# Gated mLSTM attention with a mixture of eight experts: the last two batches drained in their own order, choice counts that compare with stored steps, the first expert's down weights split in block 0

## The chip, the cores and the metric

One core of a Trainium2 chip. The metric is the device time of one execution in microseconds (us); the median of the runs is given. Engines: TensorE (PE in the rows; PEld is its weight load), VectorE (DVE), ScalarE (ACT), GpSimd (POOL), SyncE (SP). All numbers of time below are from one profiled execution, counted from the start of its span.

## The reference

The input x has 32 batches of 512 rows of 512 numbers; ctx has the same shape. Cut to what matters:

```python
x = x + tanh(g_xattn) * mlstm(layernorm(x), ctx, ctx, ...)       # 8 heads of 64
x = x + tanh(g_ffn) * ffn(layernorm(x), Wr, br, W_up, b_up, W_down, b_down)

def ffn(x, ...):                       # 16384 rows, 8 experts
    xf = x.reshape(16384, 512)
    Sm = softmax(xf @ Wr + br)         # probabilities, 16384 x 8
    G_t, idx_t = top_k(Sm.T, 2048)     # each expert chooses 2048 rows
    mid = silu(tokens @ W_up[expert // 2] + b_up)      # 512 -> 1365
    out = mid @ W_down[expert] + b_down                # 1365 -> 512
    y = zeros.at[idx].add(G * out)
```

So each expert takes the 2048 rows in which its probability is largest (on equal values the earlier row), and the output adds what the experts give for a row. The experts can't start before the probabilities of all batches are there.

## The kernel before, in words

**Two stages.** `attention` (L89) works through the batches, `experts` (L1288) through 32 blocks of 512 chosen rows, four blocks (BPE) for each expert. Each stage is one block of five instruction streams, one for each engine, ordered by hand; between streams there are only semaphores. At the end of a stage all engines meet.

**Attention** is a software pipeline: iteration i loads and norms batch i, turns q and k of batch i-1 and computes its gates, does the decays, scores and products of batch i-2, weighs the result of batch i-3 and adds it to x on GpSimd (`weigh_heads` L206: times one factor per head; `weigh_columns` L214: times the output weights Wo, then the add into xs), norms batch i-4 again (`second_norm`, ACT) into xfb, turns it on TensorE (`turn_rows`) and ACT copies it to xfT (`turned_rows`), and computes logits and probabilities of batch i-5 (`logits`, `turn_logits`, `shifted_logits`, `exponentials`, `probabilities`). The loops run NB + 5 = 37 iterations; in the last ones only the tail of this list is live. One batch of square roots a round: `row_variances` on VectorE, `rsqrt_guess` (a logarithm and an exponential) on ACT, `reciprocal_roots` (three Newton instructions and the means) on VectorE. It serves the heads of batch i-3, the first norm of batch i and the second norm of batch i-4 together.

Two banks, T[0] and T[1], carry every small product of TensorE that another engine takes. `iteration_fills` (L159) lists, for each iteration, the fills in their order, who takes each, and which bank (its last number) it uses; TensorE waits before a fill until the last one of the same bank is taken. All four xfT fills of a batch stand on bank 0, after lt.

For the last batch, 31, GpSimd weighs tile 0 only and VectorE tiles 1 to 3 (`last_rows`, L877), in the middle of iteration 34, ahead of `shifted_logits` of batch 29. SP stores in every iteration, in this order: rows of batch i-4, probabilities of batch i-5, x of batch i-3.

**The choice** (class `Select`, L1113). An expert's 16384 probabilities lie as 128x128. The 2048th largest is found two bits at a time: `steps` lists a turn, seven rounds on the upper 16 bits of the number, eight on the lower, then ties, base and four row steps that make the list of row numbers. A round is `product` (TensorE adds the counts over the partitions) and `decide` (VectorE finds the new known value and counts again in `reach`):

```python
self.step(dve.tensor_scalar(self.cand[:, :], self.threes[:, :], float(1 << bit), known[:, 0:1], ALU.mult, ALU.add))
for j in range(3):
    ins = dve.tensor_scalar(self.hit[:, j, :], values, self.cand[:, j:j + 1], self.less[:, :], ALU.is_ge, ALU.add,
                            accum_out=self.count[:, j + 1:j + 2])
```

cand holds the known value plus one, two and three steps. After the last upper round the key of the lower rounds is made (L1240 to L1244). For expert 0 the whole choice runs ahead of block 0 with nothing else on TensorE. For the others each step is put between the down matmuls of the expert before (`next_steps`, L1346).

**Weights** (`Weights`). A piece is loaded by SP into one of two raw buffers (piece m waits until piece m-2 is split), split by ACT into a high part (`hi`) and by another engine into the rest (`lo`). Expert 0 has four up and six down pieces (`first_down` = 10); all ten are split during its choice, with `lo` on GpSimd. Expert 1 and later have their down pieces split in their first block, one after each of the first steps of the up loop, with `lo` on VectorE (`down_pieces`, L1333); `lay` (L1100) then moves rows of the last chunk by three DMAs.

**A block**: 132 up matmuls in 11 groups over three banks UP, silu on ACT, the split of its result on VectorE, then four down groups of 32 matmuls over two banks DN; bias and gate on VectorE; a scatter with add by GpSimd (L1405). The rows of the next block are gathered meanwhile (L1385).

## Time and profile before

| | us |
|---|---|
| runs, median of 3 | 3284.83 (3283.53 to 3833.15) |
| the profiled execution | 3284.7 |
| its span in the profile | 3283.0 |
| mean granted clock of TensorE | 0.975 |
| last products of the attention's batch 31 begin | 1151.48 |
| attention ends, the choice's block begins | about 1195.8 |
| first list of rows ready for the gather | 1247.7 |
| first up matmul | 1258.66 |

The profiled execution's time is the same measure as the runs'; its span is 1.7 us shorter and is what all rows refer to. Mean times of a group are in ns, everything else in us.

### The profile page before, as it was taken

The page shows a single profiled execution, that of the slowest core. Times are in us where ns is not written, and L with a number is a line of the kernel's source. Part 1 is how long each engine was busy: PE and PEld are TensorE (multiplying, and loading weights), DVE is VectorE, ACT ScalarE, POOL GpSimd, SP SyncE. Part 2 cuts the span into 40 slices and gives each one's busy share as a digit, 9 for nine tenths or more (in the row PEclk, how much of TensorE's full clock was granted, in tenths as well). Part 3 has the DMA queues.
Part 4 walks back from the last instruction along what each step waited for, and adds up shares of the span by engine and source line. Part 5 has one row for each costly group of instructions (what it writes and reads, how often), then busy time and mean ns, then how long its engine had stood idle before and what let it go on. Part 6 is the DMA issues. An engine that isn't in the chain of part 4 may idle for free.

```text
span 3283.0 us, 60869 instructions
## 1 busy us (share of the span) xinstructions
PE 3054.0 (93%) x24708; PEld 2412.5 (73%) x24708; DVE 1918.8 (58%) x5481; ACT 1140.0 (35%) x1964; POOL 1079.0 (33%) x1020
## 2 busy tenths in 40 slices
PE   5899899998999927999999999999999999999998
PEld 4677777777777715777778778777778778777786
DVE  4778888888888765544545544554553554553332
ACT  3566767667676631112112112112112112211210
POOL 4465656656566541211111111121111112112111
PEclk8899999999999958999999999999999999999999
DMA  3133343433434142213223222223123223222211
GB/s 108 53 135 113 121 140 117 139 110 121 140 118 141 69 120 56 42 37 78 35 47 100 37 48 74 35 45 102 35 35 72 49 38 96 51 35 52 55 32 25
DMA packets 140064, 250.70 MB, mean 76 GB/s; under 512 B 31456, under 2 KB 31456, under 8 KB 139784
## 3 DMA queue, kind: packets, MB, share of 16 engines
q1 hardware_dynamic: 106104, 170.80, 15.4%
q0 software_dynamic: 28672, 67.65, 11.7%
q10 hardware_dynamic: 5008, 8.36, 0.8%
q8 instruction: 195, 3.19, 0.4%
q14 instruction: 85, 0.70, 0.1%
HBM read 137.23 MB, written 101.19 MB: 73 GB/s over the span
## 4 chain that ended last, share of the span: by engine, by line
PE 60%; DVE 2%; DMA 1%; issue 0%; POOL 0%; ACT 0%; POOLq 0%; ACTq 0%
PE DN L1515 29%; PE UP L1489 28%; PE TT L1459 2%; DMA w_raw<-in_L_ffn_W_down 1%; DVE c_hit L1203 0%; DVE c_cand L1201 0%; PE c_bank L1195 0%; DVE down_lo L1097 0%; PE c_bank L1187 0%; ACT z L1431 0%; DMA xg<-rows_scratch,slots 0%; POOL out_x L1405 0%; DVE c_gained L1235 0%; DVE c_key L1241 0%; POOL xg L1385 0%
## 5 line engine op out<-in xcount | busy, mean ns | idle before, releaser
L1405 POOL DMA_INDIRECT out_x<-y,slots x128 | 201.3, 1573 | 1639.2 <-DVE y L1569 1639.2
L1515 PE MATMUL DN<-down_hi,mid_hi 128*128 128x512 f32 x1408 | 578.8, 411 | 0.0
L1489 PE MATMUL UP<-xT_hi,up_hi 128*128 128x512 f32 (+1 forms) x1408 | 553.9, 393 | 2.0 <-DVE xT_lo L1526 0.9
L1489 PE MATMUL UP<-xT_hi,up_lo 128*128 128x512 f32 (+1 forms) x1408 | 555.4, 394 | 0.0
L1489 PE MATMUL UP<-xT_lo,up_hi 128*128 128x512 f32 (+1 forms) x1408 | 552.0, 392 | 0.0
L1431 ACT ACTIVATE z<-UP,bup 128x512 f32<-128x512 f32 (+1 forms) x352 | 240.9, 686 | 868.6 <-PE UP L1489 843.1
L1515 PE MATMUL DN<-down_hi,mid_lo 128*128 128x512 f32 x1280 | 505.0, 395 | 0.0
L1515 PE MATMUL DN<-down_lo,mid_hi 128*128 128x512 f32 x1280 | 504.9, 394 | 0.0
L1545 DVE CAST mid_hi<-z 128x512 fp32r<-128x512 f32 (+1 forms) x352 | 151.6, 431 | 492.3 <-ACT z L1431 489.1
L1414 ACT ACTIVATE xT_hi<-TT 128x512 fp32r<-128x512 f32 x126 | 74.9, 595 | 704.7 <-PE TT L1459 683.2
L1489 PEld LDWEIGHTS UP<-xT_hi,up_hi 128*128 128x128 f32 (+1 forms) x1408 | 260.2, 185 | 69.2 <-ACT z L1431 4.8
L1489 PEld LDWEIGHTS UP<-xT_lo,up_hi 128*128 128x128 f32 (+1 forms) x1408 | 259.7, 184 | 66.8 <-issue 0.3
L1489 PEld LDWEIGHTS UP<-xT_hi,up_lo 128*128 128x128 f32 (+1 forms) x1408 | 259.9, 185 | 65.6 <-issue 0.5
L1515 PEld LDWEIGHTS DN<-down_hi,mid_hi 128*128 128x128 f32 x1408 | 265.6, 189 | 52.2
L1515 PEld LDWEIGHTS DN<-down_hi,mid_lo 128*128 128x128 f32 x1280 | 239.8, 187 | 58.4
L1515 PEld LDWEIGHTS DN<-down_lo,mid_hi 128*128 128x128 f32 x1280 | 241.0, 188 | 46.1
L1567 DVE TENSOR_TENSOR y<-DN,bdn 128x512 f32<-128x512 f32 x128 | 88.5, 691 | 308.3 <-PE DN L1515 307.5
L1547 DVE TENSOR_TENSOR mid_lo<-z,mid_hi 128x512 fp32r<-128x512 f32 (+1 forms) x352 | 244.0, 693 | 12.1
L211 POOL TENSOR_TENSOR nsb<-nsb,rr 128x512 f32<-128x512 f32 x125 | 126.9, 1046 | 361.2 <-DVE nn L874 361.2
L900 DVE SCALAR_TENSOR_TENSOR C<-QK,C 128x512 f32<-128x512 f32 x256 | 164.3, 683 | 2.4 <-PE QK L653 1.0
L817 DVE BATCH_NORM_STATS2 st<-xs 128x6 f32<-128x512 f32 x256 | 158.2, 681 | 4.1 <-POOL xs L222 2.1
L1385 POOL DMA_INDIRECT xg<-rows_scratch,slots x128 | 140.8, 1100 | 59.1 <-issue 38.4
(246 smaller groups left out, 5133.7 us busy)
## 6 DMA issues: line engine op xcount, KB each, us to landing
xs<-in_x SPq DMA_DIRECT2D x32, 1024.0 KB, 7.7
kraw<-in_ctx SPq DMA_DIRECT2D x32, 1024.0 KB, 6.5
out_x<-xs SPq DMA_DIRECT2D x32, 1024.0 KB, 5.3
rows_scratch<-xfb SPq DMA_DIRECT2D x32, 1024.0 KB, 4.3
w_raw<-in_L_ffn_W_down SPq DMA_DIRECT2D x40, 512.0 KB, 4.4
w_raw<-in_L_ffn_W_up SPq DMA_DIRECT2D x16, 682.5 KB, 4.2
mid_hi<-mid_hi ACTq DMA_DIRECT2D x32, 86.0 KB
mid_lo<-mid_hi ACTq DMA_DIRECT2D x32, 84.0 KB
```

Of the source, the lines that this page charges most:

```text
L211: ins = eng.tensor_tensor(n, n, spread(scale[:, j, :], 2, DH), ALU.mult)
L817: dve.bn_stats(st[:, which, j, :], src[:, j, :]).then_inc(s["dchain"], 1)
L900: dve.scalar_tensor_tensor(out=c, in0=QK[:, par, :], scalar=DH ** -0.5, in1=c, op0=ALU.mult, op1=ALU.mult)\
L1385: pool.indirect_dma_start(xg[:, t, :], None, rows_v, bass.IndirectOffsetOnAxis(ap=slots[:, 4 * n + t:4 * n + t + 1], axis=0)).then_inc(s_r ...
L1405: pool.indirect_dma_start(out_rows, bass.IndirectOffsetOnAxis(ap=slots[:, m:m + 1], axis=0), y[:, t, :], None, compute_op=ALU.add).then_in ...
L1414: act.activation(xT[0][:, c, :], turned(n, c)[:, :], ACT.Copy).then_inc(s["thi"], 1)
L1431: act.activation(z[0:r, k % 2, :], UP[k % 3][0:r, :], ACT.Silu, bias=bup[0:r, e // 2, f:f + 1]).then_inc(s["z"], 1)
L1489: mm = pe.matmul(UP[k % 3][0:r, :], weights.up[wa][:, c, f * P:f * P + r], xT[xa][:, c, :], start=first, stop=(c == CH - 1 and wa == 1))
L1515: mm = pe.matmul(DN[m % 2][:, :], lhs, rhs, start=first, stop=(f == FCH - 1 and lhs is parts[-1][0]))
L1545: dve.tensor_copy(mid[0][0:r, f, :], z[0:r, k % 2, :]).then_inc(s["hi"], 1)
L1547: dve.tensor_tensor(mid[1][0:r, f, :], z[0:r, k % 2, :], mid[0][0:r, f, :].bitcast(FP32), ALU.subtract)\
L1567: dve.tensor_tensor(y[:, t, :], DN[m % 2][:, :], bdn[:, e % 2, :], ALU.add).then_inc(s["yp"], 1)
```

## The change

It touches three places.

1. **The drain.** All loops of the attention run NB + 2 iterations; what came later is written out by hand for each engine, a being batch 30 and b batch 31. TensorE's fills of xfT alternate between the banks. VectorE multiplies batch 31 with Wo pair by pair before its square sums are complete (`weigh_early`), takes the statistics of batch 30 tile by tile as GpSimd adds them, and does the second norm of tiles 1 to 3 of batch 31 itself (`last_norm`); ACT does tile 0. SP's order is rows 30, x 31, probabilities 29, rows 31, probabilities 30 and 31.
2. **The choice.** A class `Steps` holds, for each round, its step and the three multiples of it (`gain`, `reach`); GpSimd fills it at the end of its attention stream. A compare becomes one instruction that subtracts the known value and compares with the stored multiple. `gained` compares the summed counts with K - 0.5 and adds the steps reached. The key is made in two instructions.
3. **The weights.** Only the four up pieces of expert 0 are split ahead; its six down pieces go through block 0 as those of the others through their first blocks, with `lay` there too.

```diff
+            if i == NB + 2:
+                plan = [("lg", b5, 0, "act", 1), ("lt", b5, 0, "dve", 0)] + [("xfT", b4, c, "act", c % 2) for c in range(CH)]
+            if i == NB + 3:
+                plan = [("lg", b5, 0, "act", 0), ("lt", b5, 0, "dve", 1)] + [("xfT", b4, c, "act", c % 2) for c in range(CH)]
...
             @block.sync
+                store_rows(NB - 2)
+                store_x2(NB - 1)
+                store_probabilities(NB - 3)
+                store_rows(NB - 1)
+                store_probabilities(NB - 2)
+                store_probabilities(NB - 1)
...
             @block.gpsimd
+                pool.wait_ge(s["rr"], NB + 3)
+                weigh_heads(step, pool, NB - 1, slice(0, 1))
+                add_rows(pool, NB - 1, 0).then_inc(s["x2"], 1)
+                pool.wait_ge(s["x2"], NB)
+                plan.fill(pool, low[:, :])
...
             @block.scalar
+                b, a = NB - 1, NB - 2
+                numerators(b, 3)
+                squares(b, 3)
+                logit_rows(a - 1)
+                rsqrt_guess(NB + 2)
+                exponentials(a - 1)
+                second_norm(a, (0, 1, 2, 3))
+                for c in range(CH):
+                    turned_rows(a, c)
+                rsqrt_guess(NB + 3)
+                second_norm(b, (0,))
+                logit_rows(a)
+                exponentials(a)
+                for c in range(CH):
+                    turned_rows(b, c)
+                logit_rows(b)
+                exponentials(b)
...
             @block.tensor
+                product(NB - 1, 3)
+                for b in (NB - 3, NB - 2, NB - 1):
+                    logits(b)
+                    turn_logits(b)
+                    if b < NB - 1:
+                        for c in range(CH):
+                            turn_rows(b + 1, c)
...
             @block.vector
+                def weigh_early(b, p):
+                    n = nsb[:, b % 2, :, 2 * p:2 * p + 2, 0:DH]
+                    w = Wo[:, 2 * p * DH:(2 * p + 2) * DH].rearrange("p (a d) -> p a d", d=DH)
+                    step(dve.tensor_tensor(n, n, spread(w, 1, TILES), ALU.mult))
...
+                def last_norm(b):
+                    dve.wait_ge(s["rr"], b + 5)
+                    wait_filled(dve, "xfT", b - 1, CH - 1)
+                    dve.wait_ge(s_rows, 16 * b)
+                    for j in range(1, TILES):
+                        ins = dve.tensor_scalar(xfb[:, j, :], xs[:, b % XBUF, j, :], rr[:, N2 + j:N2 + j + 1],
+                                                nn[:, TILES + j:TILES + j + 1], ALU.mult, ALU.add)
+                    ins.then_inc(s["xf2v"], 1)
...
+                b, a = NB - 1, NB - 2
+                weigh_early(b, 0)
+                weigh_early(b, 1)
+                square_sums(b, 2)
+                weigh_early(b, 2)
+                for j in range(TILES - 1):
+                    dve.wait_ge(s["x2t"], j + 1)
+                    row_stats(a, j)
+                dve.wait_ge(s["x2"], a + 1)
+                row_stats(a, TILES - 1)
+                square_sums(b, 3)
+                head_variances(b)
+                row_totals()
+                row_variances(NB + 2)
+                shifted_logits(a - 1)
+                weigh_early(b, 3)
+                reciprocal_roots(NB + 2)
+
+                last_rows(b)
+                for j in range(1, TILES):
+                    row_stats(b, j)
+                dve.wait_ge(s["x2"], b + 1)
+                row_stats(b, 0)
+                row_totals()
+                row_variances(NB + 3)
+                probabilities(a - 1)
+                reciprocal_roots(NB + 3)
+                last_norm(b)
+                shifted_logits(a)
+                probabilities(a)
+                shifted_logits(b)
+                probabilities(b)
...
 class Steps:
+    def fill(self, pool, draft):
+        step = Chain(pool, self.made)
+        step(pool.memset(self.gain[:, :, :], 0.0))
+        for r, (_, bit) in enumerate(self.rounds):
+            ins = pool.memset(self.gain[:, r, 1:4], float(1 << bit))
+        step(ins)
...
+        step(pool.tensor_tensor(self.reach[:, :, :], self.gain[:, :, 1:4], spread(self.threes[:, :], 1, len(self.rounds)), ALU.mult))
...
 class Select:
+    def count_reaching(self, dve, values, r):
+        for j in range(3):
+            ins = dve.scalar_tensor_tensor(out=self.hit[:, j, :], in0=values, scalar=self.plan.gain[:, r, 0:1],
+                                           in1=self.plan.reach[:, r, j:j + 1].to_broadcast([P, P]), op0=ALU.subtract, op1=ALU.is_ge,
+                                           accum_out=self.plan.count[:, j + 1:j + 2])
         ins.then_inc(self.asked, 1)
-        dve.memset(known[:, 1:4], float(1 << bit)).then_inc(self.own, 1)
...
+            known = plan.gain[:, r + 1, 0:1] if g else self.low[:, :] if kind == "upper" else self.tail[:, :]
+            step(dve.scalar_tensor_tensor(out=self.gained[:, :], in0=bank[:, 508:512], scalar=self.K - 0.5, in1=plan.gain[:, r, :],
+                                          op0=ALU.is_ge, op1=ALU.mult, accum_out=known))
...
+                step(dve.scalar_tensor_tensor(out=self.key[:, :], in0=upper, scalar=self.low[:, :], in1=self.wrap[:, :].to_broadcast([P, P]),
+                                              op0=ALU.subtract, op1=ALU.mult, accum_out=self.junk[:, 0:1]))
+                step(dve.scalar_tensor_tensor(out=self.key[:, :], in0=lower, scalar=1.0, in1=self.key[:, :],
+                                              op0=ALU.mult, op1=ALU.add, accum_out=self.junk[:, 1:2]))
...
-        first_down = weights.upto("down", 0)
+        first = weights.upto("up", 0)
...
-            return [] if n % BPE or e == 0 else list(range(weights.upto("down", e) - (FCH + 1) // 2, weights.upto("down", e)))
+            return [] if n % BPE else list(range(weights.upto("down", e) - (FCH + 1) // 2, weights.upto("down", e)))
...
-                weights.lay(act, 0)
...
-                        if at == FCH - 3 and n and n % BPE == 0:
+                        if at == FCH - 3 and n % BPE == 0:
                             weights.lay(act, e)
```

## Rows read from the trace of the kernel before

**Rows 1.** The page: TensorE's busy time, and its granted clock in 40 slices.

```profile
PE 3054.0 (93%) x24708; PEld 2412.5 (73%) x24708; DVE 1918.8 (58%) x5481; ACT 1140.0 (35%) x1964; POOL 1079.0 (33%) x1020
...
PEclk8899999999999958999999999999999999999999
```

**Rows 2.** Busy time by stage: drain, choice, experts (length, engines, clock, DMA, GB/s).

```profile
1151.48:1195.79 44.31, 16.93 (x176) 11.81 (x175) 20.68 (x57) 14.87 (x29) 7.17 (x6) 0.56 0.27 96
1195.79:1247.73 51.94, 4.43 (x26) 2.56 (x27) 44.98 (x187) 12.56 (x11) 27.08 (x22) 0.50 0.49 134
...
1258.66:3283.00 2024.34, 2013.17 (x9061) 1592.58 (x9061) 952.13 (x2692) 363.66 (x532) 338.03 (x252) 1.00 0.25 52
```

**Rows 3.** Timeline of PE in the drain: start, us, instruction [idle before <-releaser].

```profile
1169.42 1.09 PE L589 MATMUL T<-ident,xfb 128*128 128x128 f32 x4 [13.95 <-DVE lt L836]
...
1176.70 1.94 PE L598 MATMUL T<-xfT,Wr 128*32 128x128 f32 x32 [0.78 <-ACT xfT L409]
...
1183.37 1.12 PE L589 MATMUL T<-ident,xfb 128*128 128x128 f32 x4 [3.72 <-ACT xfb L457]
```

**Rows 4.** Timeline of DVE in the drain.

```profile
1154.19 2.48 DVE L817 BATCH_NORM_STATS2 st<-xs 128x6 f32<-128x512 f32 x4 [2.11 <-POOL xs L222]
...
1160.50 3.73 DVE L211 TENSOR_TENSOR nsb<-nsb,rr 128x512 f32<-128x512 f32 x3
1164.27 2.75 DVE L218 TENSOR_TENSOR nsb<-nsb,Wo 128x512 f32<-128x512 f32 x3
1167.05 1.90 DVE L222 TENSOR_TENSOR xs<-xs,nsb 128x512 f32<-128x512 f32 x3
...
1179.48 0.20 DVE L84 SCALAR_TENSOR_TENSOR tt<-vv,rr 128x40 f32<-128x40 f32 x1 [6.28 <-ACT rr L392]
...
1194.80 0.19 DVE L843 TENSOR_TENSOR sm_all<-ex,sx 128x32 f32<-128x32 f32 x1
```

**Rows 5.** Timeline of POOL in drain and choice.

```profile
1149.54 4.62 POOL L222 TENSOR_TENSOR xs<-xs,nsb 128x512 f32<-128x512 f32 x4
...
1198.15 1.84 POOL L1176 IOTA c_slot_row<- 128x2048 f16 x1
1201.55 6.08 POOL L1097 TENSOR_TENSOR up_lo<-w_raw,up_hi 128x1365 fp32r<-128x1365 f32 x2 [1.56 <-ACT up_hi L1091]
...
1217.57 2.34 POOL L1097 TENSOR_TENSOR down_lo<-w_raw,down_hi 128x1024 fp32r<-128x1024 f32 x1 [1.69 <-ACT down_hi L1091]
```

**Rows 6.** Chain of waits in the choice: start, us, what.

```profile
1217.65 2.42 DVE c_key L1241
...
1222.68 0.24 DVE c_cand L1201
...
1222.95 1.08 DVE c_hit L1203 x6
...
1224.50 0.24 DVE c_cand L1201
```

**Rows 7.** DVE groups by form in the choice: count, busy us, mean ns, idle before.

```profile
L1201 DVE TENSOR_SCALAR c_cand<-c_threes,c_gain 128x3 f32<-128x3 f32 x15 | 13.4, 893 | 0.5
```

**Rows 8.** DVE groups by form from 1262 us to the end.

```profile
L1203 DVE TENSOR_SCALAR_CACHE_REDUCE c_hit<-c_key,c_cand,c_less 128x128 f16<-128x128 f32 x168 | 59.4, 404 | 2.1
...
L1241 DVE SCALAR_TENSOR_TENSOR c_key<-c_V,c_gain 128x128 f32<-128x128 uint16 x7 | 2.4, 341 | 0.0
```

**Rows 9.** Timeline of ACT in block 4.

```profile
1525.16 1.06 ACT L1091 ACTIVATE down_hi<-w_raw 128x1024 fp32r<-128x1024 f32 x1 [3.70 <-DMA w_raw<-in_L_ffn_W_down]
```

**Rows 10.** Busy time in expert blocks 0, 1, 4 and 16, as rows 2.

```profile
1258.66:1323.73 65.07, 65.07 (x285) 50.82 (x286) 32.51 (x116) 10.44 (x17) 8.72 (x7) 0.97 0.19 37
1323.73:1386.83 63.10, 63.10 (x286) 49.43 (x284) 32.51 (x122) 9.85 (x15) 10.88 (x8) 1.00 0.20 37
1512.42:1575.90 63.48, 63.44 (x286) 49.45 (x284) 38.15 (x120) 14.88 (x21) 11.65 (x8) 1.00 0.39 96
2268.74:2332.34 63.60, 63.60 (x285) 49.47 (x284) 38.14 (x120) 14.88 (x21) 11.65 (x8) 1.00 0.37 90
```

More of the change, by code:

```diff
@@ L219, in weigh_columns, with add_rows @@
             step(ins)
-            for j in range(tiles.start, tiles.stop):
-                xb = xs[:, b % XBUF, j, :].rearrange("p (h d) -> p h d", d=DH)
-                ins = eng.tensor_tensor(xb, xb, nsb[:, b % 2, j, :, 0:DH], ALU.add)
-            return ins
+        def add_rows(eng, b, j):
+            xb = xs[:, b % XBUF, j, :].rearrange("p (h d) -> p h d", d=DH)
+            return eng.tensor_tensor(xb, xb, nsb[:, b % 2, j, :, 0:DH], ALU.add)
         with nc.Block() as block:
@@ L1132, in __init__ @@
         self.groups = [list(range(a, a + TILES)) for a in range(0, self.KC, TILES)]
-        self.steps = [("turn", 0)] + [("upper", k) for k in range(self.TOP_BIT - self.LOWER - 1, -1, -2)] \
-            + [("lower", k) for k in range(self.LOWER - 2, -1, -2)] + [("ties", 0), ("base", 0)] \
-            + [("rows", g) for g in range(len(self.groups))]
-        self.V = sb("V", [P, P]); self.key = sb("key", [P, P]); self.beyond = sb("beyond", [P, P])
+        self.rounds = [("upper", k) for k in range(self.TOP_BIT - self.LOWER - 1, -1, -2)] \
+            + [("lower", k) for k in range(self.LOWER - 2, -1, -2)]
@@ new lines, in __init__ @@
+        self.steps = [("turn", 0)] + self.rounds + [("ties", 0), ("base", 0)] + [("rows", g) for g in range(len(self.groups))]
+        R = len(self.rounds)
+        self.gain = sb("gain", [P, R, 4]); self.reach = sb("reach", [P, R, 3])
+        self.threes = sb("threes", [P, 3])
+        self.count = sb("count", [P, 4], BF16)
+        self.onesb = sb("onesb", [P, P], BF16)
+        self.made = ctx.enter_context(nc.semaphore("c_made"))
+    def fill(self, pool, draft):
[3 more added lines that the diff above has]
+            ins = pool.memset(self.gain[:, r, 1:4], float(1 << bit))
+        step(ins)
+        step(pool.iota(self.threes[:, :], pattern=[[1, 3]], base=1, channel_multiplier=0, allow_small_or_imprecise_dtypes=True))
+        step(pool.tensor_tensor(self.reach[:, :, :], self.gain[:, :, 1:4], spread(self.threes[:, :], 1, len(self.rounds)), ALU.mult))
+        pool.memset(self.count[:, 0:1], float(P)).then_inc(self.made, 1)
+        step.line.n += 1
+        step(pool.memset(draft, 1.0))
+        step(pool.tensor_copy(self.onesb[:, :], draft))
@@ L1226, in decide @@
         if kind == "turn":
-            step(dve.memset(self.gain[0][:, :], 0.0))
             step(dve.tensor_copy(self.V[:, :], bank[:, 0:P]))
             if e == 0:
-                dve.wait_ge(self.made, 5)
-            self.reach(dve, upper, self.gain[0], self.steps[i + 1][1])
+                dve.wait_ge(plan.made, plan.MADE)
+            self.count_reaching(dve, upper, 0)
         elif kind in ("upper", "lower"):
-            old, new = self.gain[(i - 1) % 2], self.gain[i % 2]
-            dve.wait_ge(self.own, step.line.n)
@@ L1243, in decide @@
[L1243 to L1248 removed]
+                if e == 0:
+                    dve.wait_ge(self.laid, self.LAID)
@@ L1388, in _ @@
                 select.constants(pool)
-                for m in range(first_down):
+                for m in range(first):
                     weights.lo(pool, m)
@@ L1414, in turn_hi @@
                     act.activation(xT[0][:, c, :], turned(n, c)[:, :], ACT.Copy).then_inc(s["thi"], 1)
[L1416 removed]
+                for m in range(first):
                     weights.hi(act, m)
```

174 lines of the change are left out of this document (87 added, 87 removed).

## The prediction, made before the result was known

> **What bounds the kernel now.** I read the page first, then busy time by stage, then the chain of waits, then the timelines of single engines between 1149 and 1262 us. The page shows TensorE at 93% and at full clock nearly everywhere, except for one slice of half clock between 1149 and 1231 us [rows 1]. The stages say where that lies [rows 2]. From 1258.66 us to the end TensorE is busy for 2013 of 2024 us: the expert stage is bound by its matmuls, and no edit changes their number. The 44.3 us before 1195.79, in which the last batches of the attention drain, hold 16.9 us of TensorE work, and the 51.9 us after it, in which the first expert's rows are chosen, hold 4.4. Those 96 us are latency: a gain or a loss there moves the end one for one. The change touches both, and the first expert block behind them.
>
> **Drain of the last two batches.** Behind the logits of batch 29 TensorE stands still for 13.95 us, until 1169.42, when VectorE has taken them (L836) [rows 3]. VectorE has them late in its order: it first weighs and adds three tiles of batch 31, from 1160.50 to 1168.9 [rows 4]. Then the four turns of batch 30 go one at a time, because all use one bank: 7.3 us from 1169.42 to the logits at 1176.70, 1.80 each where TensorE's share is 1.1 [rows 3]. ACT takes up the guess for batch 31's norm only after them, so VectorE waits 6.28 us for it [rows 4].
>
> The new order, worked forward:
> - The roots of round NB+2 are ready at 1160.5 now [rows 4]. Ahead of them VectorE gets three early products with Wo, and one behind the variances, and they alternate with GpSimd's four adds, which run from 1149.5 [rows 5]: a tensor_tensor of VectorE on two SBUF tiles takes 1.24 beside GpSimd (3.73 for 3) and 0.63 alone [rows 4, 5]. The row statistics now start tile by tile instead of after all four adds. Stepping through it, the roots come 1.1 us later: 1161.6.
> - Batch 31's three tiles: the products with Wo (2.75) are gone from there. Left are 3.73 for the head weights, 1.9 for the adds, and 0.6 for meeting GpSimd's add and its new fills: 1167.8.
> - Statistics 2.48, totals and variances 0.6: 1170.9. ACT's guess follows at once, since batch 30's copies are over by then (norm of 30 until 1164.6, with 3.0 for its four rows as from 1180.4 to the turn at 1183.37 now, four turns at about 1.1 each on two banks): 0.55, and the Newton steps 0.9: 1172.4. So the 6.28 us wait is gone.
> - Three rows of the last norm on VectorE, about 0.5 each (the 0.49 of L1569, same shape and operation), beside one on ACT: 1173.9. That batch 30's logits (about 1.9, from 1169.7) and their turn are done by then costs nothing; the store of batch 30, for which the last norm also waits, is issued at 1164.6.
> - From batch 31's first turn to its last probability it takes 11.6 now (1183.37 to 1194.99) [rows 3, 4]. Two banks save three times 0.7: 9.5. End 1183.5 instead of 1195.0.
>
> That is 11.5 us gained. If the alternation costs each DVE product one more GpSimd instruction, 8 are left; if turns pair up better and the early products cost nothing, 14.
>
> **The choice of the first expert.** A round is a count on VectorE, a 4-column matmul and a decision, with 15 rounds in it. An unhindered round takes 1.82 us, from one candidate instruction (1222.68) to the next (1224.50), and 1.08 of it are the three compares [rows 6]. The change:
> - takes the candidate instruction out of every round: 15 x 0.27 = 4.0 gained;
> - with it go its stalls. The 15 candidates took 13.4 us together [rows 7], 9.8 more than 15 x 0.24. They ended when a GpSimd instruction ended (the long iota, the splits up_lo and down_lo) [rows 5];
> - makes the key in two instructions instead of copy, three 128x128 passes and a memset. Now this is 5.2 us, from 1217.49 to 1222.66, 2.42 of them in one scalar_tensor_tensor that started with GpSimd's split at 1217.57 [rows 5, 6]; with nothing beside it the same instruction takes 0.34 [rows 8]. New: 2 x 0.45. 4.3 gained;
> - but makes each compare a scalar_tensor_tensor with two SBUF tiles. The old compare ran through splits untouched (0.40 with 0.33 between starts, in every case [rows 8]); the new one has the form of c_key, the one that was blocked. So GpSimd's splits now stop the compares, nearly from beginning to end: 6.08 for two up pieces, then 2.6 and 2.6, and perhaps the iota, 1.84 [rows 5]. The six down pieces are no longer there. Stepping the rounds through these windows (one compare gets in between two splits) I get 9.4 without the iota and 11.0 with it: given back.
>
> With the iota 4.0 + 9.8 + 4.3 - 11.0 = 7.1, and a little more for the memset ahead of the first count; without it 8.7. I take 8.0, between the two. Bounds: compares that are not blocked, 18; compares at half pace, 0.13 each more for their 128 elements, 45 x 0.13 = 6 less: 2.
>
> The Trainium skill bears on two of these steps. "SBUF — State Buffer" (section "SBUF: two separate sides") says that VectorE with two SBUF inputs and a GpSimd instruction that reads SBUF exclude each other for a whole instruction; c_key at 2.42 beside 0.34 agrees, and the iota, which reads nothing, would by this rule stop no compare: by it the choice gains 8.7 rather than 7.1. "Vector Engine (DVE) Microarchitecture Reference" (section "Points that are easy to get wrong") says that a scalar_tensor_tensor with two SBUF sources that aren't bf16 runs at half throughput, since no port is left for the accumulator. The trace has no such instruction with an accumulator; c_key without one, 0.34, isn't halved.
>
> GpSimd's constants for the counts move into the drain, where it idles from 1165 us on: nothing gained but 0.1, since the first product came right behind the first count anyway.
>
> **The first expert's down weights.** Their six pieces leave the choice and are split by ACT and VectorE in block 0, as in the first block of every other expert. There ACT waits on loads (3.70 us before the third piece, [rows 9]), yet the blocks take 63.48 and 63.60 us where one without pieces takes 63.10 [rows 10]; two others were at 63.1. TensorE has three output banks ahead of it, and that hides it. Block 0 begins at half clock and takes 65.07 now [rows 10], which slows its demand, not its loads. I take 0.3 lost, between 0 and 1.5. The seven later choices run beside the down matmuls, which wait for no count today; 0.27 off each decision changes nothing.
>
> **Sum.** 11.5 + 8.0 - 0.3 = 19.2. The profiled execution took 3284.7 (span 3283.0 and 1.7 around it), so it goes to 3265.5; the median of the three runs, 3284.83, lies 0.1 above it: 3265.6.
>
> **Rivals.**
> - Free compares (0.1): they pass the splits as the old ones did. For it speaks that both have an accumulator and that 45 old ones were never blocked; against it the 2.42 of c_key. Choice 18 instead of 8: 3255.6.
> - Half-pace compares (0.12): 6 more in the choice, 3271.6. This is the page's rule above.
> - The drain yields half (0.12): ACT or TensorE, in a strict order of their own, become late where I have them idle, or two SBUF products meet more of GpSimd: 5.7 instead of 11.5, 3271.4.
> - Slower than before (0.02): block 0 starves. Two raw buffers carry six pieces, so the last two pairs each pay a full load. It decides from the point where a load takes longer than the cover; beyond it each us of load costs about 2. For 19.2 lost a load must take some 10 us more than the 7 behind the 3.70 us wait, with block 0 at 85 us and the whole at 3286 or more. The other first blocks, with scatter and gather beside their loads, speak against it.
>
> **How the numbers follow.** The forecast has 0.64, the rivals 0.36 together. For the forecast alone the range is 3261 to 3270. Taking in the half-pace and the half-drain case with a little beyond, and the free compares, gives 3255 to 3274. A change of over 2% (about what a measurement of this kernel can tell from none) would need 66 us of the 96, or as much lost: 0.01 each, and 0.98 for within.
>
> **What would show it.** Right: in the drain the gap of TensorE after the logits of batch 29 ends with the norm of batch 30, near 1165, turns come 1.1 apart, and attention ends near 1183.5. In the choice, compares of 2.5 to 3 us stand exactly where GpSimd's four up_lo lie, and the others are 0.33 apart; the first gather is issued near 1228. Block 0 takes 65 to 66 us, and all later blocks are as they were. Wrong: compares 0.45 apart or more, roots of round NB+2 beyond 1163, block 0 over 67 us, or any later block longer.

## The result and the profile after

| | before | after |
|---|---|---|
| runs, median | 3283.53 (3279.67 to 3833.15, five) | 3258.58 (3256.45 to 3259.18, five) |
| ratio, with its 95% interval | | 0.9926 (0.991 to 0.9941) |
| the profiled execution, its span | 3284.7, 3283.0 | 3257.32, 3255.4 |
| mean granted clock of TensorE | 0.975 | 0.98 |

The change takes 24.95 us off the median, 0.74% by the ratio: within 2%, but well clear of no change by the interval. Of the five runs of before, 3833.15 was a slow one; without it their median is 3282.76 and the gain 24.2. The forecast was 3265.6; the result lies 7.0 below it, inside the wide range of 3255 to 3274 but below the 3261 to 3270 given for the forecast alone. It is nearer to the rival of free compares (3255.6), so the time alone would have pointed to the wrong mechanism; the profile decides. The spans of the two profiled executions differ by 27.6, and that is what the account below divides. The boundaries in the table are starts of instructions in the timelines, and for block 0 the end of its last matmul.

| stage | before | after | gained | forecast |
|---|---|---|---|---|
| start to the last products of batch 31 | 1151.48 | 1150.84 | 0.64 | 0 |
| drain, to the choice's first turn | 44.35 | 30.54 | 13.81 | 11.5 |
| choice, to its first list of rows | 51.65 | 40.71 | 10.94 | 8.0 |
| first list to first up matmul | 11.18 | 10.90 | 0.28 | 0 |
| block 0 | 65.07 | 63.33 | 1.74 | -0.3 |
| the rest | 1959.27 | 1959.08 | 0.19 | 0 |

The page of after, answering [rows 1]: TensorE's busy time and its granted clock in 40 slices.

```profile
PE 3048.6 (94%) x24708; PEld 2411.2 (74%) x24708; DVE 1870.8 (57%) x5235; ACT 1140.2 (35%) x1961; POOL 1064.8 (33%) x1029
...
PEclk8899999999999969999999999999999999999999
```

Busy time by stage in after, answering [rows 2] and [rows 10]: drain, choice, block 0, all experts (length, PE, PEld, DVE, ACT, POOL, clock, DMA share, GB/s).

```profile
1150.84:1181.38 30.54, 14.60 (x177) 11.46 (x176) 21.39 (x60) 12.79 (x26) 8.72 (x27) 0.64 0.39 139
1181.38:1222.09 40.71, 4.24 (x23) 2.29 (x23) 34.46 (x154) 6.65 (x5) 14.10 (x11) 0.50 0.39 103
1232.99:1296.32 63.33, 63.33 (x285) 49.80 (x286) 35.80 (x110) 15.63 (x23) 9.35 (x7) 1.00 0.34 82
1232.99:3255.40 2022.41, 2011.39 (x9061) 1592.46 (x9061) 912.03 (x2474) 369.88 (x538) 334.87 (x252) 1.00 0.25 53
```

TensorE's busy share hardly moves (93 to 94%), and its expert work is as long as it was (2013.17 and 2011.39). Where before has two slices at 5 and 8, one at 6 is left: the low stretch is shorter, not gone. Of the 27.6 us, 24.75 lie in the two stages in which TensorE mostly waits, and 1.7 where the first block starts; the 0.64 and 0.19 at both ends are no more than single executions differ by.

TensorE in the drain of after, from its timeline, answering [rows 3] (start, us, instruction, idle before it and what ended it).

```profile
1162.71 3.77 PE L638 MATMUL T<-ident,xfb 128*128 128x128 f32 x16 [7.88 <-ACT xfb L485]
...
1171.35 0.45 PE L655 MATMUL T<-ident,lg 128*128 128x128 f32 x1 [3.01 <-ACT lg L495]
1171.69 3.74 PE L638 MATMUL T<-ident,xfb 128*128 128x128 f32 x16
1176.21 1.94 PE L647 MATMUL T<-xfT,Wr 128*32 128x128 f32 x32 [0.78 <-ACT xfT L437]
```

The gap of 13.95 us before batch 30's turns is 7.88 and ends with ACT's norm of batch 30, as forecast. The four turns go as one group of 16 transposes in 3.77: 0.94 apart where they were 1.80.

VectorE in the drain of after, from its timeline, answering [rows 4].

```profile
1148.79 2.27 DVE L938 TENSOR_TENSOR nsb<-nsb,Wo 128x512 f32<-128x512 f32 x2
...
1151.69 0.96 DVE L938 TENSOR_TENSOR nsb<-nsb,Wo 128x512 f32<-128x512 f32 x1
...
1158.10 0.68 DVE L938 TENSOR_TENSOR nsb<-nsb,Wo 128x512 f32<-128x512 f32 x1
...
1159.72 3.73 DVE L223 TENSOR_TENSOR nsb<-nsb,rr 128x512 f32<-128x512 f32 x3
1163.48 2.05 DVE L236 TENSOR_TENSOR xs<-xs,nsb 128x512 f32<-128x512 f32 x3
...
1170.14 1.46 DVE L967 TENSOR_SCALAR xfb<-xs,rr,nn 128x512 f32<-128x512 f32 x3
...
1180.35 0.19 DVE L900 TENSOR_TENSOR sm_all<-ex,sx 128x32 f32<-128x32 f32 x1
```

The first two early products take 2.27 together (the second alone 1.55), the third 0.96, the fourth 0.68. The fourth is issued between variances and roots, and batch 31's tiles begin right behind it, at 1159.72. No wait of 6.28 us stands before the Newton steps any more: batch 31's norm starts at 1170.14, and its last probability ends at 1180.54.

GpSimd in drain and choice of after, from its timeline, answering [rows 5].

```profile
1148.89 5.94 POOL L236 TENSOR_TENSOR xs<-xs,nsb 128x512 f32<-128x512 f32 x4
...
1182.43 1.84 POOL L1313 IOTA c_slot_row<- 128x2048 f16 x1
1187.57 6.13 POOL L1215 TENSOR_TENSOR up_lo<-w_raw,up_hi 128x1365 fp32r<-128x1365 f32 x2 [3.29 <-ACT up_hi L1209]
1195.96 2.60 POOL L1215 TENSOR_TENSOR up_lo<-w_raw,up_hi 128x1365 fp32r<-128x1365 f32 x1 [2.26 <-ACT up_hi L1209]
1199.65 2.61 POOL L1215 TENSOR_TENSOR up_lo<-w_raw,up_hi 128x1365 fp32r<-128x1365 f32 x1 [1.09 <-ACT up_hi L1209]
```

VectorE in the choice of after, from its timeline: the compare beside the long iota, the three that met a split, and the first key instruction.

```profile
1182.47 0.35 DVE L1343 SCALAR_TENSOR_TENSOR c_hit<-c_V,c_gain,c_reach 128x128 f16<-128x128 uint16 x1
...
1187.77 3.01 DVE L1343 SCALAR_TENSOR_TENSOR c_hit<-c_V,c_gain,c_reach 128x128 f16<-128x128 uint16 x1
...
1190.71 3.13 DVE L1343 SCALAR_TENSOR_TENSOR c_hit<-c_V,c_gain,c_reach 128x128 f16<-128x128 uint16 x1
...
1196.01 2.69 DVE L1343 SCALAR_TENSOR_TENSOR c_hit<-c_V,c_gain,c_reach 128x128 f16<-128x128 uint16 x1
...
1199.75 2.66 DVE L1379 SCALAR_TENSOR_TENSOR c_key<-c_V,c_low,c_wrap 128x128 f32<-128x128 uint16 x1
```

This is the picture to learn. The compare at 1182.47 lies inside GpSimd's iota (1182.43 to 1184.27) and takes 0.35. The compares at 1187.77 and 1190.71 start in the pair of splits that begins at 1187.57 and ends at 1193.70, and take 3.01 and 3.13, to the end of the one split and to the end of the other; the compare at 1196.01 and the key at 1199.75 end with the next two splits.

VectorE's groups by form in the expert stage of after, answering [rows 8] (count, busy us, mean ns).

```profile
L1343 DVE SCALAR_TENSOR_TENSOR c_hit<-c_key,c_gain,c_reach 128x128 f16<-128x128 f32 x168 | 50.3, 350 | 2.0
...
L1379 DVE SCALAR_TENSOR_TENSOR c_key<-c_V,c_low,c_wrap 128x128 f32<-128x128 uint16 x7 | 2.5, 352 | 0.3
```

The new compare with nothing beside it takes 350 ns with its accumulator, the old one 404.

### The profile page after: what moved, and what is told of

Its sections match the earlier page's. It is cut to its first block, busy times and chain, and to the rows that moved or that the text cites. A ratio compares the mean times of both kernels' runs of the same rounds, so it can differ in the third digit from the quotient of the medians.

```text
span 3255.4 us, 60512 instructions
## 1 busy us (share of the span) xinstructions
PE 3048.6 (94%) x24708; PEld 2411.2 (74%) x24708; DVE 1870.8 (57%) x5235; ACT 1140.2 (35%) x1961; POOL 1064.8 (33%) x1029
## 4 chain that ended last, share of the span: by engine, by line
PE 60%; DVE 1%; DMA 1%; issue 0%; ACT 0%; POOL 0%; POOLq 0%; ACTq 0%
PE DN L1647 30%; PE UP L1621 28%; PE TT L1594 2%; DMA w_raw<-in_L_ffn_W_down 1%; DVE c_hit L1343 1%; PE c_bank L1336 0%; DVE down_lo L1215 0%; PE c_bank L1326 0%; ACT z L1566 0%; DMA xg<-rows_scratch,slots 0%; POOL out_x L1541 0%; DVE c_key L1379 0%; DVE c_gained L1372 0%; POOL xg L1521 0%; DVE mid_lo L1679 0%
## 5 line engine op out<-in xcount | busy, mean ns | idle before, releaser
L1647 PEld LDWEIGHTS DN<-down_lo,mid_hi 128*128 128x128 f32 x1280 | 241.2, 188 | 45.8
L702 PE MATMUL QK<-qT,kT 64*128 64x128 f32 x2048 | 153.2, 290 | 1.6 <-DVE C L988 1.6
```

Of the source, the lines that this page charges most:

```text
L702: mm = pe.matmul(QK[:, par, jj], kT[r, b % 2, p, jj], qT[r, b % 2, p, jj], start=True, stop=True)
L1647: mm = pe.matmul(DN[m % 2][:, :], lhs, rhs, start=first, stop=(f == FCH - 1 and lhs is parts[-1][0]))
```

## The experiments

Stage lengths of every run, read at the same instructions as above. The time is that of the profiled execution; single executions of the kernel before took 3278.5 and 3279.0 beside e1 to e7, and the median of 25 was 3283.65 beside e8 to e11.

| run | drain | choice | list to up | block 0 | span | time |
|---|---|---|---|---|---|---|
| before | 44.35 | 51.65 | 11.18 | 65.07 | 3283.0 | 3284.7 |
| after | 30.54 | 40.71 | 10.90 | 63.33 | 3255.4 | 3257.3 |
| e1_drain_alone | 29.36 | 48.12 | 11.04 | 65.22 | 3262.7 | 3264.6 |
| e2_ten_pieces | 30.53 | 49.01 | 11.10 | 64.91 | 3267.1 | 3269.0 |
| e3_old_choice | 30.36 | 45.81 | 10.93 | 64.88 | 3261.9 | 3263.9 |
| e4_one_bank | 34.34 | 40.14 | 10.95 | 63.42 | 3260.8 | 3262.7 |
| e5_wo_late | 30.58 | 40.16 | 11.01 | 63.32 | 3306.4 | 3308.4 |
| e6_psum_table | 30.52 | 30.46 | 10.88 | 63.40 | 3244.8 | 3246.8 |
| e7_before_warm | 44.31 | 51.90 | 10.92 | 64.87 | 3284.0 | 3286.1 |
| e8_before_warm2 | 44.30 | 49.17 | 11.57 | 63.28 | 3281.8 | 3283.5 |
| e9_psum_warm | 30.53 | 30.45 | 11.57 | 63.31 | 3247.1 | 3249.2 |
| e10_psum_table_timed | 30.53 | 30.46 | 10.84 | 63.38 | 3245.1 | 3247.1 |
| e11_psum_warm_all | 28.75 | 30.47 | 11.62 | 63.32 | 3241.9 | 3243.9 |

In e5 the attention ahead of the drain ran 47 us longer in this execution; its stage lengths are used, its time is not. The 3243.9 of e11 is the shortest of its 12 executions.

Each stage length is that of one execution, so its spread has to be known. The choice of after took 40.71, 40.16 and 40.14 in three runs that have the same choice (after, e5, e4), and that of e6 took 30.45 to 30.47 in four. The old choice with ten pieces took 48.12 to 51.90 in four; the reason is below.

**e1_drain_alone.** The attention of after without the constants of part 2 (`Steps.fill`), and everything behind the attention as in before.

```diff
-def attention(nc, io, NB, dram, sm_all, tg, consts, stored, plan):
+def attention(nc, io, NB, dram, sm_all, tg, consts, stored):
...
-                plan.fill(pool, low[:, :])
```

> The first part alone, the choice and the weights as before. If the three parts add up, the stage from the last products of batch 31 to the choice's first turn goes from 44.4 to about 30.5 us as in the changed kernel, the choice (first turn to first list) stays at 51.9, block 0 at 65.1; all in all 13.8 us under the kernel before. If the drain's gain had needed the constants moved out of the choice or the new loads behind it, the stage is over 32 or the choice over 53.

The drain took 29.36: part 1 does its work without the others. The 1.2 us less than in after are the last logits, 1.08 instead of 1.94 us long at full clock, with what follows. The surprise is the choice: the same code as before, on the same ten pieces, took 48.12 instead of 51.65. Its 15 candidates took 12.2 us instead of 13.4 [rows 7], and the first scalar_tensor_tensor of the key 1.8 instead of 2.42 [rows 6]. So the old choice has no single length. Its rounds are the same, and what differs is where in a split each of its blocked instructions starts. The third candidate decides most of it. It starts 5.78 us behind the choice's first turn in all of before, e1, e3, e7 and e8. GpSimd's first split starts at 5.72 in before, 5.79 in e7 and 5.60 in e3, and this candidate takes 3.03, 3.09 and 2.92; the split starts at 5.92 in e1 and 6.28 in e8, and the candidate takes 0.23. Here it is in before and in e8, from their timelines of VectorE:

```profile
1201.61 3.03 DVE L1201 TENSOR_SCALAR c_cand<-c_threes,c_gain 128x3 f32<-128x3 f32 x1
```

```profile
1202.54 0.23 DVE L1201 TENSOR_SCALAR c_cand<-c_threes,c_gain 128x3 f32<-128x3 f32 x1
```

The first instruction of the key starts 21.73 us behind the choice's first turn in before, and 19.18 in e8 and 18.56 in e1. Up to there before, e7 and e8 hold the same instructions, so this is a difference between executions and not between kernels: the split follows ACT's `hi`, and ACT waits for the load of the weights. The profiled execution of before drew the long case, and up to 3.5 of the 10.9 us by which the choice became shorter are owed to that.

**e2_ten_pieces.** After, with part 3 undone.

```diff
-        first = weights.upto("up", 0)
+        first = weights.upto("down", 0)
-            return [] if n % BPE else list(range(weights.upto("down", e) - (FCH + 1) // 2, weights.upto("down", e)))
+            return [] if n % BPE or e == 0 else list(range(weights.upto("down", e) - (FCH + 1) // 2, weights.upto("down", e)))
+                weights.lay(act, 0)
...
```

> The changed kernel with the third part undone: all ten pieces are split by GpSimd during the choice. If a split on GpSimd holds up every compare that reads two SBUF tiles, the six down splits (five of some 2.1 us and one of 1.1) come on top: the choice goes from 40.9 to about 50 us, and compares of about 2.3 us stand at each down split. If only the loads mattered, or the split held up just the candidates of the old form, the choice stays at 41 to 42. Block 0 about 0.2 shorter either way.

The choice took 49.01. VectorE in the choice of e2, from its timeline:

```profile
1204.38 2.37 DVE L1343 SCALAR_TENSOR_TENSOR c_hit<-c_key,c_gain,c_reach 128x128 f16<-128x128 f32 x1
...
1207.79 1.50 DVE L1343 SCALAR_TENSOR_TENSOR c_hit<-c_key,c_gain,c_reach 128x128 f16<-128x128 f32 x1
...
1211.73 2.07 DVE L1343 SCALAR_TENSOR_TENSOR c_hit<-c_key,c_gain,c_reach 128x128 f16<-128x128 f32 x1
```

In after there is no compare over 0.35 behind the key. With ten pieces the compares of the lower rounds meet the splits of the down weights as well, and 8.3 us of the choice (49.01 - 40.71) come from part 3 alone.

**e3_old_choice.** Parts 1 and 3, with the compares, candidates and key of before. The edit is shown against e1.

```diff
-        first_down = weights.upto("down", 0)
+        first_down = weights.upto("up", 0)
-                weights.lay(act, 0)
-                        if at == FCH - 3 and n and n % BPE == 0:
+                        if at == FCH - 3 and n % BPE == 0:
```

> The drain and the weights as changed, the choice in its old form (candidates, old compares). The stalls at down splits go (4.2 at the key, 2.1 at candidates, by the trace of before), those at the iota and the four up splits stay (some 7.7): the choice goes from 51.9 to about 45.5. If the gain in the choice was all the new compares' own, it stays at 51.9.

The choice took 45.81. VectorE's groups by form in the choice of e3:

```profile
L1318 DVE TENSOR_SCALAR c_cand<-c_threes,c_gain 128x3 f32<-128x3 f32 x15 | 11.3, 754 | 0.5
```

The 15 candidates still took 11.3 us. With e1 and e2 this makes a square: old counts with ten pieces 48.1 (51.7 in before), with four 45.8; new counts with ten 49.0, with four 40.7. By themselves the new counts gain 2.6 at most, or lose 0.9. Moving the pieces gains 2.3 for the old counts if e1 is the start, but e1 drew the short case and e3 the long one; from before, which drew the long one too, it is 5.8. For the new counts it is 8.3. The two parts alone sum to 8.5 at most, and together they take off 10.9. Block 0 carries the six pieces here and took 64.88, with 64.91 in e2, which has none there: the pieces cost nothing.

**e4_one_bank.** After, with all xfT fills of the drain on bank 0.

```diff
-[("xfT", b4, c, "act", c % 2) for c in range(CH)]
+[("xfT", b4, c, "act", 0) for c in range(CH)]
```

> The changed kernel with all turns of batches 30 and 31 on one bank. A turn then takes 1.80 us instead of 0.94: batch 31's way from first turn to last probability goes from 8.85 to 11.5 (2.6 lost), and batch 30's copies end at about 1169.9 instead of 1167.1, 1.2 after ACT's guess for the last norm was due, so 3.8 lost in all. If batch 30's copies are hidden, 2.6; if the banks are not what spaces the turns, 0.

The drain took 34.34, 3.80 more. TensorE's turns in e4, from its timeline:

```profile
1175.58 1.11 PE L638 MATMUL T<-ident,xfb 128*128 128x128 f32 x4 [0.69 <-ACT xfT L437]
...
1181.07 1.94 PE L647 MATMUL T<-xfT,Wr 128*32 128x128 f32 x32 [0.78 <-ACT xfT L437]
```

They start 1.78 to 1.80 apart again, as in [rows 3], where two banks have 0.94. Of the 13.8 us of the drain, the banks are 3.8.

**e5_wo_late.** After, with batch 31's products with Wo behind the head weights, as in before.

```diff
-                weigh_early(b, 0)
-                weigh_early(b, 1)
...
-                weigh_early(b, 2)
...
-                weigh_early(b, 3)
...
+                    weigh_columns(step, dve, b, slice(1, TILES))
```

> The changed kernel with batch 31's products with Wo back behind the head weights (VectorE tiles 1 to 3, GpSimd tile 0). The roots of round NB+2 then come earlier by what the early products cost (about 0.7 for the fourth and 1.3 for holding up GpSimd's adds, so at 1157.7 instead of 1159.7), and the rows of batch 31 later by 2.75 or a little more: 1 to 1.5 us lost on the whole. If the early products cost nothing, 2.8 to 3.5 lost; if they cost what they save, 0.

The drain took 30.58, no longer than in after. VectorE in the drain of e5, from its timeline:

```profile
1205.46 3.73 DVE L223 TENSOR_TENSOR nsb<-nsb,rr 128x512 f32<-128x512 f32 x3
1209.22 2.75 DVE L230 TENSOR_TENSOR nsb<-nsb,Wo 128x512 f32<-128x512 f32 x3
...
1218.60 1.46 DVE L969 TENSOR_SCALAR xfb<-xs,rr,nn 128x512 f32<-128x512 f32 x3
```

The products cost 2.75 here again, and batch 31's norm ends 1.0 us later behind the last products of batch 31 than in after. That microsecond doesn't show in the stage: here the last logits ran at full clock, 1.08 instead of 1.94, and the turn behind them was 0.14 shorter. So the early products are worth about 1.0, less than the 2.75 they take off the tail, since they come back ahead of the roots.

**e6_psum_table.** After, with expert 0's stored multiples, the key's factor and the key's first half in two idle PSUM banks; ACT copies the first two there ahead of its splits.

```diff
+            at = self.table[:, 3 * r + j:3 * r + j + 1] if e == 0 else self.plan.reach[:, r, j:j + 1]
-  in1=self.plan.reach[:, r, j:j + 1].to_broadcast([P, P])
+  in1=at.to_broadcast([P, P])
+  act.activation(UP[2][:, 0:45], plan.reach[:, :, :].rearrange("p r j -> p (r j)"), ACT.Copy).then_inc(select.tabled, 1)
+  act.activation(UP[1][:, 64:65], select.wrap[:, :], ACT.Copy).then_inc(select.tabled, 1)
```

> The changed kernel, but for expert 0 the compares read their step, and the key its factor and its first half, from PSUM instead of SBUF, so each has one SBUF tile only. If the lock between two SBUF reads of VectorE and GpSimd's splits is the cause, every compare takes 0.3 to 0.4 and the 10 us of stalls go: the choice goes from 40.9 to about 31, unless the PSUM operand makes each compare some 0.06 longer (33). The four splits then run at 2.6 each. If any compare is held up by a split whatever it reads, it stays at 41.

The choice took 30.46, 10.25 less than in after. VectorE's groups by form in the choice of e6, and below them GpSimd's timeline:

```profile
L1346 DVE SCALAR_TENSOR_TENSOR c_hit<-c_key,c_gain,UP 128x128 f16<-128x128 f32 x24 | 7.1, 345 | 0.3
L1346 DVE SCALAR_TENSOR_TENSOR c_hit<-c_V,c_gain,UP 128x128 f16<-128x128 uint16 x21 | 6.2, 345 | 0.2
...
L1384 DVE SCALAR_TENSOR_TENSOR UP<-c_V,c_low,UP 128x128 f32<-128x128 uint16 x1 | 0.4, 356 | 0.0
```

```profile
1186.01 6.08 POOL L1215 TENSOR_TENSOR up_lo<-w_raw,up_hi 128x1365 fp32r<-128x1365 f32 x2 [2.91 <-ACT up_hi L1209]
1194.59 2.60 POOL L1215 TENSOR_TENSOR up_lo<-w_raw,up_hi 128x1365 fp32r<-128x1365 f32 x1 [2.50 <-ACT up_hi L1209]
1197.87 2.60 POOL L1215 TENSOR_TENSOR up_lo<-w_raw,up_hi 128x1365 fp32r<-128x1365 f32 x1 [0.68 <-ACT up_hi L1209]
```

GpSimd's four splits are there, as long as ever (6.08, 2.60, 2.60), and all 45 compares average 345 ns. That the second source of a compare is read from PSUM instead of SBUF is the whole difference, so the blocking is one of SBUF access by two engines, not of order or semaphores. The compares and the key lost 7.8 and 2.3 to it in after, 10.1 together, and 10.25 came back.

**e7_before_warm, e8_before_warm2.** Before, with spare transposes on TensorE ahead of block 0: in e7 eight behind each of the four row steps of the choice, in e8 8, 10, 14 and 16 and some behind each gathered tile.

```diff
                     select.product(pe, 0, i)
+                    if select.steps[i][0] == "rows":
+                        for _ in range((8, 10, 14, 16)[select.steps[i][1]]):
+                            pe.transpose(UP[1][:, 0:P], ident[:, :], ident[:, :])
```

> The kernel before, with eight more transposes on TensorE behind each of the four row steps of expert 0's choice (into a bank that is not in use), so that TensorE is busy from some 8 us earlier. If block 0 is 1.8 us shorter in the changed kernel only since the clock had risen when it began, block 0 goes from 65.1 to 63.2 here, with granted clock 1.0 from its first matmul. If it was the moved down pieces or the lay-out DMAs, it stays at 65.

> The kernel before with the gaps of TensorE filled more closely than in e7_before_warm: 8, 10, 14 and 16 spare transposes behind the four row steps, 3 behind each of the first three tiles of gathered rows and 10 behind the last, right up to the first up matmul. In e7_before_warm the clock rose 9.5 us ahead of block 0 and fell again 0.5 us into it. If it fell because of the gaps, it stays up here and block 0 takes 63.3 to 63.5 us instead of 65. If the clock has nothing to do with block 0's length, or falls all the same, 65.

Granted clock around the start of block 0, from busy time in stretches of 2 us, first of before, then of after, e7 and e8:

```profile
1258.66:1260.66 2.00, 2.00 (x5) 1.34 (x6) 1.79 (x4) 0.60 (x2) 0.00 (x0) 0.50 0.07 14
...
1262.66:1264.66 2.00, 2.00 (x11) 1.52 (x10) 0.48 (x2) 0.68 (x1) 1.70 (x2) 1.00 0.77 212
```

```profile
1230.99:1232.99 2.00, 0.75 (x5) 0.54 (x5) 0.84 (x2) 1.47 (x4) 0.00 (x0) 0.94 0.00 0
1232.99:1234.99 2.00, 2.00 (x9) 1.38 (x10) 1.78 (x4) 0.60 (x2) 0.00 (x0) 1.00 0.00 0
```

```profile
1257.31:1259.31 2.00, 0.66 (x5) 0.46 (x5) 0.84 (x2) 1.47 (x4) 0.00 (x0) 1.00 0.00 0
1259.31:1261.31 2.00, 2.00 (x6) 1.34 (x7) 1.78 (x4) 0.59 (x2) 0.00 (x0) 0.63 0.08 15
```

```profile
1257.50:1259.50 2.00, 2.00 (x9) 1.37 (x10) 1.78 (x4) 0.60 (x2) 0.00 (x0) 1.00 0.08 15
1259.50:1261.50 2.00, 2.00 (x11) 1.51 (x10) 0.28 (x1) 0.68 (x1) 1.13 (x2) 1.00 0.38 107
```

In before the clock is at 0.50 (1.2 GHz) when block 0 starts and at 1.00 (2.4 GHz) only 4 us later. In after it rises while the last of the four gathered tiles is turned, some 1.8 us ahead of the block (the mean of 0.94 leaves 0.24 us of the 2 at half clock). e7 missed: the clock was up ahead of the block (1257.31), but the mean of 0.63 in its first 2 us puts the fall 0.5 us into it, and block 0 took 64.87. It says nothing for either theory. e8 held the clock at 1.00, and block 0 took 63.28 with no pieces in it, as in after with them. Over all profiles the length of block 0 goes with this alone: 63.28 to 63.42 where it starts at full clock and keeps it, 64.87 to 65.22 where it doesn't.

**e9_psum_warm.** e6 with the transposes of e8.

> The kernel of e6_psum_table with the fillings of e8_before_warm2 behind its choice. Block 0 was at full clock there without them (63.4), so nothing is gained there; the turns of the gathered rows at full clock give up to 0.3. Span 0.3 under that of e6_psum_table within what the attention stage varies by. If the fillings hold up the row steps, the stretch from the first list to the first up matmul goes over 11.2.

Nothing was gained: e6 started block 0 at full clock anyway (63.40), and the transposes behind the gathered tiles hold up the first up matmul by 0.7 us (11.57 for 10.88).

**e10_psum_table_timed.** e6 again, timed.

> The kernel of e6_psum_table again, timed. The changed kernel stands 24.9 us under the one before; with the choice at 30.5 instead of 40.7 us it should stand 34 to 36 under it, a ratio of 0.989 to 0.990. If the stalls come back elsewhere (splits late, block 0 waiting for up pieces), it is at 25.

The median was 3248.03, 35.6 below the 3283.65 of the kernel before beside it; ratio 0.9907 (0.9883 to 0.9931). This beats the kernel before. Against after the intervals of the two ratios overlap, so there the times alone decide less than the stage: 30.46 for 40.71, with nothing lost behind it.

**e11_psum_warm_all.** e9 with spare transposes in the drain too, 40 while TensorE waits for the norm of batch 30 and 12 before batch 30's logits are turned.

```diff
+                    if b == NB - 3:
+                        for _ in range(40):
+                            pe.transpose(QK[:, 0, 0:P], ident[:, :], ident[:, :])
```

> The kernel of e9_psum_warm with 40 spare transposes in TensorE's wait for the norm of batch 30 and 12 ahead of the turn of batch 30's logits, so that its clock may stay up in the drain. Turns are spaced by ACT's copies and gain 0.1 each at most; the last logits take 1.08 instead of 1.94 and what follows 0.2 less: the drain goes from 30.5 to some 29.2 us, the whole 1.3 under e10_psum_table_timed. If the clock falls all the same, the spare transposes last 8.5 us at half clock and hold up the turns of batch 30 by 0.6 us or more: drain 30.5 to 31.5.

TensorE in the drain of e11, from its timeline:

```profile
1168.59 2.70 PE L638 MATMUL T<-ident,xfb 128*128 128x128 f32 x16
1172.07 1.08 PE L647 MATMUL T<-xfT,Wr 128*32 128x128 f32 x32 [0.78 <-ACT xfT L437]
```

The last turns take 2.70 instead of 3.74 and the last logits 1.08 instead of 1.94, and the drain is 1.8 us shorter, more than the 1.3 expected. The 40 transposes didn't keep the clock up for batch 30: its turns took 3.77 as in after, and its logits 1.94 where after has 1.08. Of the gain 0.8 goes in the 11.62 ahead of block 0, and timed the kernel was no faster than e10: median 3249.75, ratio 0.9924 (0.9892 to 0.9956). Keeping TensorE warm pays too little here to be seen in the time.

## Why the prediction was right, and where its sizes were off

**What bounds the kernel** was right. Only the 96 us between attention and block 0 shrank, one for one, and the expert stage kept its length but for its first microseconds.

**Drain: forecast 11.5, measured 13.8.** The steps came in their order; three terms were mis-sized.
- Roots of round NB+2, "1.1 us later: 1161.6". They end at 1159.7; with the 0.64 by which the stage began earlier that is 1160.3 on the clock of before, or 1.3 sooner than forecast. I had each early product wait for one of GpSimd's adds. Of the three, only the second (1.55) and a little the third (0.96) did, and GpSimd's adds became longer (5.94 for 4.62); row statistics tile by tile hid most of that.
- Batch 31's tiles, 6.2 from the roots to the end of the adds by forecast: 1159.7 to 1165.5, so 5.8, or 0.35 less. From there to the end of the norm it took 6.1, as forecast.
- From batch 31's first turn to its last probability, 9.5: it took 8.85 (1171.69 to 1180.54). I had turns 1.1 apart with "three times 0.7" saved; without the wait between them they also overlap, at 0.94. e4 gives the two banks 3.8 for two batches, 0.6 for every one of six waits. This is 0.65 less, and with 1.3 and 0.35 the whole 2.3.
- The wait of 6.28 us is gone, as forecast, and batch 30's logits cost nothing. But they weren't done as early as forecast: they end at 1168.34, ACT takes them only behind its guess and its row of the last norm, and their turn starts at 1171.35, just ahead of batch 31's turns at 1171.69.

**Choice: forecast 8.0, measured 10.9.** The mechanism was right and seen where it was put: compares of 2.7 to 3.1 us stand exactly at three of the four up_lo, and the key's first instruction at the last. By the forecast's own terms:
- candidates 4.0 and their stalls 9.8: as forecast, the instructions are gone. That the stalls were real is shown by e1 and e3 (12.2 and 11.3 us of candidates). Their size was partly luck: I took the 9.8, and the 51.65 of the whole choice, from one execution as if they belonged to the kernel, and other executions of the same rounds took 48.12 to 51.90.
- key 4.3: it took 3.0 (from 1199.75 to the first lower compare) instead of 0.9, since a split blocked its first instruction too. 2.2 gained.
- given back to the splits, 9.4 to 11.0: three compares lost 3.01 + 3.13 + 2.69 - 3 x 0.35 = 7.8. The last split fell on the key instead, and with its 2.3 the splits took back 10.1, within the forecast.
- not in the sum: compares start 0.27 apart, not 0.33 as the old ones. 45 x 0.055 = 2.5 gained.

Together 4.0 + 9.8 + 2.2 - 7.8 + 2.5 = 10.7, for 10.9 measured. So the term that the forecast lacked is the shorter compare: I had them 0.33 apart like the old ones. The open point between 7.1 and 8.7, the iota, is decided. The candidate of before that met it took 1.34 us, as its timeline row shows:

```profile
1198.67 1.34 DVE L1201 TENSOR_SCALAR c_cand<-c_threes,c_gain 128x3 f32<-128x3 f32 x1
```

while the compares of after beside the same iota take 0.35. The Trainium skill, "SBUF — State Buffer" (section "SBUF: two separate sides"), said so: two SBUF inputs on VectorE exclude a GpSimd instruction that reads SBUF, and the iota reads none. e6 agrees with the same rule from the other side, with one input in PSUM.

**Rivals.** Free compares fell: e2 shows them blocked six more times, and e6 shows what they would have given, 10.25 more. Half-pace compares fell: 350 ns over 168 compares, and 352 for the key with its accumulator, are 9 and 11 more than the 341 of the key without one [rows 8], where 130 were feared; and with one source in PSUM they take 345 (e6). Here the Trainium skill, "Vector Engine (DVE) Microarchitecture Reference" (section "Points that are easy to get wrong"), and the measurement differ, and the measurement decides: a scalar_tensor_tensor with two 4-byte SBUF sources and an accumulator isn't halved. The half drain fell: ACT and TensorE were not late. Block 0 did not starve. Of the signs named ahead, compares of 2.7 to 3.1 us stood at three of the four up_lo and the key at the fourth, but attention ended at 1181.2 on the clock of before and not 1183.5, turns were 0.94 apart and not 1.1, free compares 0.27 apart and not 0.33, and block 0 took 63.33 and not 65 to 66.

**Block 0: forecast 0.3 lost, measured 1.74 gained.** The step that failed is "block 0 begins at half clock and takes 65.07 now": I took the clock at its start as fixed. The pieces cost nothing (e3 beside e2); the clock is the 1.74 (e8). What raises it a few microseconds earlier in after than in before isn't settled: e7 raised it and lost it again. Without spare transposes it was at 1.00 at the start of block 0 in the five profiles that have both the new counts and four pieces (after, e4, e5, e6, e10), and at 0.50 in the four that have not (before, e1, e2, e3).

## What to carry to other kernels

A VectorE instruction with two SBUF inputs stands still until the GpSimd instruction beside it, which reads SBUF, has ended (2.66 to 3.13 us instead of 0.35 in after), and the length of a latency-bound chain on VectorE then hangs on what GpSimd happens to run. Before rewriting such a chain, look which of its operands could lie in an idle PSUM bank (10.25 us for two small copies here), and which GpSimd work can go behind it (8.3 us). It isn't the whole rule: the old candidate, with one tensor in SBUF, was stopped as well. A stage that hangs on such meetings differs between executions (48.12 to 51.90 us for the same rounds), so take its length from more than one before a forecast subtracts from it. Price a combination of edits as a combination: the new counts alone were worth between -0.9 and 2.6, and with the pieces moved 5.1 (45.81 to 40.71).

## What was unexpected of the hardware

- A compare that subtracts and compares two tensors with an accumulator takes 350 ns and starts 0.27 us after the one before; the old compare, a tensor_scalar with two operands read per partition and an accumulator, takes 404 and 0.33. That isn't a matter of the instruction's kind alone: c_over, the same kind on 128x128 with one such operand and a constant, takes 346 to 348.
- A candidate of 3 columns, with one tensor in SBUF, stood still beside an iota (1.34 us), where the compare with two SBUF sources did not (0.35).
- The old choice, with the same rounds and pieces, took 51.65 us in before, 51.90 in e7, 49.17 in e8 and 48.12 in e1. Whether GpSimd's first split has started by the third candidate, to within 0.01 us, separates the long cases from the short ones in all of them; that start wasn't set on purpose in a run.
- Whether the first expert block starts at full clock (63.3 us) or half (64.9 to 65.2) differs between kernels that are the same from there on (before, e7 and e8), and what raises the clock in time wasn't found.
